# L1's merge: gathers of mixed rows one per turn, no barrier behind its weights, and L2's row numbers made at the merge's head

## The reference, cut to what matters

```python
h_local = layer_norm(elu(agg / denom + x + gat_b), ln_local_g, ln_local_b)
y = mamba(x[perm], ...)                       # a scan over the nodes sorted by degree
h_attn = layer_norm(x + y[inv], ln_global_g, ln_global_b)
gate = sigmoid(h_local @ wl.T + h_attn @ wg.T)
h = gate * h_local + (1.0 - gate) * h_attn
ff = relu(h @ ff1_w.T + ff1_b) @ ff2_w.T + ff2_b
out = layer_norm(h + ff, ln2_g, ln2_b)        # added to the residual, then normed for L2
```

## Time and profile before

| what | value |
| --- | --- |
| time, median of 3 runs | 8131.84 us (8129.35 to 8138.65) |
| profiled execution: time, span | 8120.78 us, 8118.8 us |
| busy of the span: PE, DVE, ACT, POOL | 5456.7, 5255.1, 3258.1, 4542.0 us |
| merge of L1, from barrier to barrier | 5036.2 to 5620.9 us |
| passes of L2 and L3 | 5620.9 us to the end |

### The profile page before, as it was taken

The page is one execution under the profiler, slowest core; times in us unless marked ns, Lnnn a source line. Parts: engine busy times, 40 slices in busy tenths (PEclk is TensorE's granted clock), DMA queues, the critical chain, the costliest instruction groups (busy, mean ns, idle before and its releaser), DMA issues. The chain is left out here.

```text
span 8118.8 us, 108950 instructions
## 1 busy us (share of the span) xinstructions
PE 5456.7 (67%) x20075; PEld 3427.6 (42%) x20075; DVE 5255.1 (65%) x11331; ACT 3258.1 (40%) x10998; POOL 4542.0 (56%) x4375
## 2 busy tenths in 40 slices
PE   4657788888888346477777775575566665566664
PEld 4523344444444222144444443464344443344443
DVE  7678588888888535689888895564455553333332
ACT  1224566666666224378787884342000000000000
POOL 4240366666664332077777773323777775777774
PEclk9988899999999557689899997797788887788887
DMA  7123577777776652377777776222344445344445
GB/s 254 25 68 110 192 243 240 245 243 241 244 243 184 215 152 82 108 235 246 240 242 244 243 238 158 67 67 71 115 141 142 142 142 96 112 136 135 136 136 89
DMA packets 485564, 1352.16 MB, mean 167 GB/s; under 512 B 131335, under 2 KB 225547, under 8 KB 484586
## 3 DMA queue, kind: packets, MB, share of 16 engines
q0 software_dynamic: 237920, 837.96, 35.4%
q1 hardware_dynamic: 204668, 441.41, 16.2%
q10 hardware_dynamic: 42668, 69.51, 2.7%
HBM read 1133.35 MB, written 546.45 MB: 207 GB/s over the span
## 5 line engine op out<-in xcount | busy, mean ns | idle before, releaser
L1190 POOL DMA_INDIRECT rows_e<-bundle,unit_src x1856 | 1777.8, 958 | 649.2 <-issue 544.9
L1211 PE MATMUL acc_e<-rows_e,hot_e 128*128 128x256 f32 x3712 | 1219.9, 478 | 906.8 <-DMA rows_e<-bundle,unit_src 733.6
L967 POOL DMA_INDIRECT rows_e<-table,unit_src x928 | 1145.6, 1235 | 707.3 <-POOLq L238 320.2
L608 POOL DMA_INDIRECT rows_e<-table,unit_src x928 | 1023.2, 1103 | 844.9 <-PE acc_e L797 465.0
L797 PE MATMUL acc_e<-rows_e,hot_e 128*128 128x512 f32 (+1 forms) x3712 | 1341.2, 511 | 174.5 <-DVE rows_e L779 99.5
L1211 PEld LDWEIGHTS acc_e<-rows_e,hot_e 128*128 128x128 f32 x3712 | 825.9, 237 | 1269.5 <-issue 587.2
L786 ACT ACTIVATE rows_e<-rows_e 128x64 f32<-128x64 f32 x4640 | 1118.9, 333 | 1.9
L797 PEld LDWEIGHTS acc_e<-rows_e,hot_e 128*128 128x128 f32 x3712 | 698.8, 196 | 748.6 <-issue 606.2
L1053 ACT ACTIVATE rows_e<-rows_e 128x64 f32<-128x64 f32 x3712 | 920.0, 333 | 3.8
L1220 DVE SCALAR_TENSOR_TENSOR sums_e<-sums_e,unit_keep,acc_e 128x256 f32<-128x256 f32 x928 | 442.8, 477 | 734.1 <-PE acc_e L1211 728.8
L2353 ACT ACTIVATE turned_f<-turn_f 128x512 f32<-128x512 f32 x98 | 58.5, 597 | 1890.2 <-PE turn_f L2351 1869.7
(11 more groups left out here) (437 smaller groups left out, 8541.4 us busy)
## 6 DMA issues: line engine op xcount, KB each, us to landing
bc<-bc_rows SPq DMA_DIRECT2D x226, 896.0 KB
summed<-sums_e SPq DMA_DIRECT2D x464, 390.0 KB
bundle<-sums_e SPq DMA_DIRECT2D x928, 128.0 KB
summed<-sums_e SPq DMA_DIRECT2D x464, 130.5 KB
given_f<-bundle ACTq DMA_DIRECT2D x98, 384.0 KB
rows_e<-table,unit_src POOLq DMA_INDIRECT x1856, 4.9
rows_e<-bundle,unit_src POOLq DMA_INDIRECT x1856, 2.7
summed<-zeros POOLq DMA_DIRECT2D x50, 390.0 KB, 17.8
```

Of the source, the lines that this page charges most:

```text
L608: pool.indirect_dma_start(self.rows[:, v, e, :], None, table, bass.IndirectOffsetOnAxis(unit_src[:, u, e:e + 1], 0)).then_inc(self.landed[ ...
L967: pool.indirect_dma_start(self.rows[:, v, e, :], None, self.tab, bass.IndirectOffsetOnAxis(unit_src[:, u, e:e + 1], 0)).then_inc(self.land ...
L1190: pool.indirect_dma_start(self.rows[:, v, e, :], None, self.tab, bass.IndirectOffsetOnAxis(unit_src[:, u, e:e + 1], 0)).then_inc(self.land ...
L1211: mm = pe.matmul(self.acc[:, v % 2, 0:D], self.hot[:, v % self.SUMS, e, :], self.rows[:, v, e, :], start=(e == 0), stop=(e == 1))
```

## The change

The barrier behind the 13 weight loads goes; the semaphore is now called `weights_here`, and DVE, ACT and PE wait for it at one place, inside the first job, in front of the step that adds `gat_b`. The 49 gathers become a generator that `in_lanes` calls once after every turn, so that they stand in POOL's queue between the steps of the lanes, in turns 0 to 48. `unit_src` is turned into L2's row numbers at the head of the merge. After the chain's step for `top` only ACT waits. At the head of L2 the six loads count on `weights_here` too, PE and DVE alone wait for them, and POOL waits for nothing.

```diff
-        merge_loaded = sem("merge_loaded")
+        weights_here = sem("weights_here")
...
-                      ).then_inc(merge_loaded, 16)
-        settle()
+                      ).then_inc(weights_here, 16)
+        all_loaded = 16 * (len(names) + len(sides) + 5)
...
-            for t in range(T):
-                pool.indirect_dma_start(y_all[:, t, :], None, sorted_y, bass.IndirectOffsetOnAxis(rank_i[:, t:t + 1], 0)
-                                        ).then_inc(returned[t // PART_OF], 16)
+
+            def return_rows():
+
+                for t in range(T):
+                    yield pool.indirect_dma_start(y_all[:, t, :], None, sorted_y,
+                                                  bass.IndirectOffsetOnAxis(rank_i[:, t:t + 1], 0)
+                                                  ).then_inc(returned[t // PART_OF], 16)
+
...
+            chain.step(dve, lambda: dve.tensor_scalar(unit_src[:, :, :], unit_src[:, :, :], 3, 1, ALU.mult, ALU.add))
             chain.step(dve, lambda: dve.tensor_scalar(top[:, :], top_neg[:, :], -1.0, None, ALU.mult))
...
-            for e in (sp, pool, pe, dve, act):
-                chain.wait(e)
-                e.wait_ge(merge_loaded, 16 * (len(names) + len(sides) + 5))
+            chain.wait(act)
...
                 yield ch.step(dve, lambda: dve.tensor_tensor(l3, l3, h3, ALU.add))
+                if b0 == 0:
+                    for e in (dve, act, pe):
+                        e.wait_ge(weights_here, all_loaded)
                 yield ch.step(dve, lambda: dve.tensor_tensor(l3, l3, bv("gat_b"), ALU.add))
...
-            in_lanes(lanes, merge, 8)
+            in_lanes(lanes, merge, 8, return_rows(), 1)
...
-            chain.dma(sp, l1, l2, l3, l4, l5, l6)
+            for load in (l1, l2, l3, l4, l5, l6):
+                load().then_inc(weights_here, 16)
+            for e in (pe, dve):
+                e.wait_ge(weights_here, all_loaded + 16 * 6)
             chain.step(dve, lambda: dve.tensor_tensor(b1[:, :], b1[:, :], b2[:, :], ALU.add))
-            chain.step(dve, lambda: dve.tensor_scalar(unit_src[:, :, :], unit_src[:, :, :], 3, 1, ALU.mult, ALU.add))
-            for e in (sp, pool, pe, dve, act):
-                chain.wait(e)
+            chain.wait(dve)
```

More of the change, by code:

```diff
@@ L2217, in graph_stack_kernel @@
         vecs = {}
-        merge_loaded = sem("merge_loaded")
+        weights_here = sem("weights_here")
         for n in names:
             vecs[n] = lsb(f"v_{n}", [P, D])
-            act.dma_start(vecs[n][:, :], a[f"L1_gnn_{n}"].partition_broadcast(P)).then_inc(merge_loaded, 16)
+            act.dma_start(vecs[n][:, :], a[f"L1_gnn_{n}"].partition_broadcast(P)).then_inc(weights_here, 16)
         for n in sides:
@@ L2224, in graph_stack_kernel @@
             act.dma_start(vecs[n][:, :], a[f"L1_gnn_{n}"].rearrange("(c p) -> p c", p=P), allow_slow_non_contiguous=True
-                          ).then_inc(merge_loaded, 16)
+                          ).then_inc(weights_here, 16)
         wl, wg, f1, f2 = (lsb(n, [P, r // P, c]) for n, r, c in (("wl", D, D), ("wg", D, D), ("f1", D, 2 * D), ("f2", 2 * D, D)))
         for v, n in ((wl, "wl"), (wg, "wg"), (f1, "ff1_w"), (f2, "ff2_w")):
-            act.dma_start(v[:, :, :], a[f"L1_gnn_{n}"].rearrange("(c p) n -> p c n", p=P)).then_inc(merge_loaded, 16)
+            act.dma_start(v[:, :, :], a[f"L1_gnn_{n}"].rearrange("(c p) n -> p c n", p=P)).then_inc(weights_here, 16)
         fb = lsb("fb", [P, 2 * D // P])
         act.dma_start(fb[:, :], a["L1_gnn_ff1_b"].rearrange("(c p) -> p c", p=P), allow_slow_non_contiguous=True
-                      ).then_inc(merge_loaded, 16)
-        settle()
+                      ).then_inc(weights_here, 16)
+        all_loaded = 16 * (len(names) + len(sides) + 5)
         with ExitStack() as local:
```

## The result

The changed kernel takes 8050.48 us in the median of 6 runs (8034.48 to 8086.71), the kernel before 8130.6 (8114.63 to 8147.13). The ratio is 0.9911, 95% interval 0.9895 to 0.9927: some 72 us less, 59 to 85. The medians by themselves are 80.1 us apart; the text goes by the ratio. I had forecast a gain of 48.8 us and the range 8067 to 8105.

The account below looks back on a forecast made before the run. An empty ramp of some 50 us behind POOL's queue of gathers, and POOL's stream pacing the passes, were taken as the bound. Merge 53.1 - 11.4 = 41.7 plus L2's head 7.1 gave 48.8 us: 8083, range 8067 to 8105.

Parts of the forecast that it names:

- The start of the stream: POOL's first gather in the merge: 0.74 us behind the first release, at 5036.95, 7.2 us earlier.
- First power: Lane 0's first power, turn 16, behind 16 gathers and lane 1's two loads: 5058.5, 53.1 us earlier; POOL decides narrowly.
- (b): Weights in the merge's ramp: 2.1 MB extra traffic at 375 GB/s, 5.6 us later, in by 5054.0; power possible at 5058.0.
- What the gathers take back: 33 gathers among the powers, turns 16 to 48: each interval the larger of old length and POOL's work; 11.4 us lost.
- fifth rival: Slower: every gather from turn 0 takes a longer slot; gain zero at 2.45 us, -0.2% at 2.8; chance 0.02.
- Behind turn 51: Rest of the merge: from turn 49 both kernels run the same steps, tail and closing barrier included.
- Head of L2: L2's first gather at 5621.6 instead of 5628.77, POOL not waiting for row numbers: gain 7.1 us, kept to the end.
- The full price: Rival: each of 33 merge gathers waits for one DVE operation, slot 1.94, excesses 27.8 us, time 8099.4; chance 0.16.
- the case in which nothing is absorbed: Rival: every gather of turns 16 to 48 lengthens its turn, 41.3 us; gain 18.9, time 8112.9; chance 0.05.
- Late weights: Rival: traffic delays weights to 5064, first power 9.6 us later, time 8092.6; chance 0.12 together with a slower clock.
- TensorE's clock: Rival: stretched ramp keeps PE's clock lower, one piece 7.8 us longer, time 8090.8; chance 0.12 together with late weights.
- The rule of the shared port: VectorE and GpSimd exclude each other, so a merge gather could wait out one DVE operation of 0.69 us; chance 0.16.

Follow-up runs that it names:

- one_piece: The changed kernel, but the 49 gathers issued in one piece ahead of the merge as before; barrier gone, L2's head new. Ratio 0.9981 against the kernel before.
- sparse: The changed kernel with gathers thinned out: 10 in turns 0 to 18, then one every fourth turn. Ratio 0.994 against the kernel before.
- bias_first: The changed kernel, DVE waiting for the bias alone before the bias add, all three engines for other weights only before lane 0's first transposes. Ratio 0.9937.
- head_only: The kernel before with only L2's head changed: row numbers made at the merge's head, POOL not waiting; merge as before. Ratio 0.9992.
- again: The changed kernel unaltered, run a second time against the kernel before. 8066.36 us, ratio 0.991.
- before_pad8: The kernel before with 8 small extra POOL instructions at the very start. Ratio 1.0 (0.9986 to 1.0014).

## Why the prediction was wrong

**The start of the stream** was right: 0.74 us behind the release in both places, 7.2 us gained by the barrier (`one_piece`: 68.2 instead of 75.4 us).

**First power.** Forecast 53.1 us earlier against the release, measured 75.4 - 25.6 = 49.8. The failing term is (b): the weights were in 3.7 us later than put. Its count of bytes was short: it added 4 gathers to the 4 that ran beside the loads before, but by its own slot POOL issues some 13 of them by 17.8 us, with lane 1's loads (0.5 MB) among them. The trace has 3.6 MB more than before instead of 2.1, and by the prediction's 375 GB/s that is 9.7 us; the weights were in 9.3 us later. That bytes are all of it is not shown: the last of the 13 issues ended 11.8 us behind the release instead of 6.5, and in `sparse`, with 8 instead of 16 gathers ahead of the wait's end, the weights were in only 1.1 us earlier. `bias_first` takes the wait away and the power comes at 22.5.

**What the gathers take back.** Forecast 11.4 us, measured from the first power to turn 51 57.2 instead of 50.8: 6.4. The slots were right: the intervals of 11.5, 3.6, 9.7, 10.9 and 3.7 us stand against 11.6, 3.6, 10.2, 10.5 and 3.6 by my terms at 1.35 us. The rule that joined them was wrong. I never let an interval fall below its old length; but the one from 32 to 33 took 2.0 instead of 5.0 us and that from 41 to 48 11.2 instead of 13.0, since DVE and PE had done their part while POOL was busy with the interval before. Taken over the whole stretch from turn 16 to 48, POOL's work by the prediction's fifth rival, 9.0 + 32 x 1.35 = 52.2 us, meets the measured 52.6. The two errors nearly cancel: 49.8 - 6.4 = 43.4 against 41.7. That the merge came out so close is partly luck.

**Behind turn 51** both kernels were to be alike: 456.9 and 458.5 us, yes.

**Head of L2**: 7.1 forecast, 6.8 in the profile of `head_only`, whose ratio of 0.9992 (0.9982 to 1.0001) agrees but cannot show it alone.

**The rivals.** The gathers did grow beside DVE, but little: the median of the 49 is 0.955 us, the mean 1.01, the longest 1.43. The full price (27.8 us) and the case in which nothing is absorbed are refuted by the 6.4 us. Late weights: shown, at 3.3 us of the first power and not 9.6. TensorE's clock: in the stretch from turn 41 to 48 (5096.2 to 5107.4 us) it was granted in full again, 1.00, as in the kernel before, so that rival did not come. The rule of the shared port (the Trainium skill, "SBUF — State Buffer", section "SBUF: two separate sides"), by which one of the two engines waits out the other's instruction, agrees with the few longer gathers; most kept 0.95 to 0.97 us while DVE was busy 7.2 of 11.2 us (5054.8 to 5066). A price that decides anything no run here shows.

**What failed** is the sum's last step: it put everything outside the two seams at the same time as before, without a reason beyond the same code. The runs show in its place that the passes of L2 and L3, apart from L2's head, take about 10 us less (L3's 1243.5 to 1245.3 us instead of 1248.9 to 1250.6, L2's 5 us less as well), since their 1856 gathers take 5 ns less each. Why they do is open. Seams and passes together give 45 + 7 + 10 = 62 us, inside the measured 59 to 85; the seams alone, 52, are outside. `sparse` is the counter-check: its merge gained 584.7 - 546.3 = 38.4 us, its head 7, its gathers are at 953 ns, and it measured 0.994, 49 us (38 to 59): nothing is left over. For the changed kernel the middle of the first interval leaves another 10 us, which single profiles can't place; by the medians of `again` (61.9 us) nothing is left. The chance of 0.07 that I gave to a gain above 51 us rested on better overlap in the merge, which is at most a small part of what came. The range was too narrow on the fast side: for what lies outside the seams it allowed the run-to-run spread and no change at all.

## What to carry to other kernels

A batch of independent transfers at the head of an in-order queue costs its whole length when the first steps of a lane stand behind it; handed out one per turn, the 61 us of it cost 6 here behind the first power, and the part ahead of that ran beside loads that had to be waited for anyway. Thinning the same transfers out further, into the flowing part, won nothing here. When transfers are let go together, count all that will be under way by the time the awaited one lands, at the new pace of issue. When two engines take turns as the bound, sum over stretches and not interval by interval, since work deferred in one interval is already done in the next.

## What the runs showed of the hardware that was not expected

The gathers of one and the same instruction had medians of 946 to 957 ns in different programs and series, and with 1856 of them the passes that they pace were some 10 us shorter, with no change to their code.

In the last two series the kernel before took 8751 and 8757 us instead of 8126 to 8132. The passes of L2 and L3 made most of it: 1519 and 1475 us in `before_pad8`. There POOL waited for PE and for others, unlike in the earlier trace rows (same view, whole passes):

```profile
POOL rows_e L1192 <- issue: 488.0, 1548, 2.0
POOL rows_e L1192 <- PE acc_e L1213: 342.8, 179, 8.4
POOL rows_e L1192 <- remote: 236.3, 126, 4.4
```

The granted clock was 0.70 of full in the stretch 5800 to 6800 us, against 0.84 in the kernel before as first profiled. What makes such a condition was not tried. The change was worth about the same share there, 0.9925 to 0.9937 against 0.991 with overlapping intervals, though its merge gained less, 549.1 and 550.5 us against 581.2 to 586.9.
